# Two attention layers on one core: maxima run 40 units ahead instead of 36, and TensorE's program written out without a loop

## The reference

```
xn  = group_norm(x) * gamma + beta
qkv = w_qkv @ xn + b_qkv                      # per head q, k, v of 32 rows
m   = softmax_t( (q*scale)^T (k*scale) )      # 1024 x 1024 for each of 8 heads
a   = m @ v
out = x + w_proj @ a + b_proj                 # the second layer does the same with its own weights
```

## Time and profile before

| | us |
|---|---|
| median of 3 runs (2229.60 to 2244.59) | 2239.12 |
| the profiled execution | 2236.67 |
| its span, first to last instruction | 2234.9 |
| TensorE busy in the span | 2123.1 (95%) |
| GpSimd busy | 1790.2 (80%) |
| VectorE busy | 1700.2 (76%) |
| ScalarE busy | 1243.4 (56%) |
| mean granted TensorE clock (1 is 2.4 GHz) | 0.974 |

### The profile page before, as it was taken

One profiled execution on the slowest core, in us unless ns is written; L12 is line 12 of the kernel. 1 busy time (PEld: TensorE's weight loads), 2 busy tenths in 40 slices (PEclk: granted clock), 3 DMA queues, 4 the chain that ended last, 5 costly groups with the idle time before them and its releaser, 6 DMA issues.

```text
span 2234.9 us, 41842 instructions
## 1 busy us (share of the span) xinstructions
PE 2123.1 (95%) x10552; PEld 1156.9 (52%) x10552; DVE 1700.2 (76%) x2896; ACT 1243.4 (56%) x2321; POOL 1790.2 (80%) x567
## 2 busy tenths in 40 slices
PE   5999999999999999999999999999999999999998
PEld 2455555555555555455554555545455554555542
DVE  3788777787877778777877878877787787878872
ACT  2455656565555655555555555655556555565554
POOL 2498788797887988878987888978889788889885
PEclk8899999999999999999999999999999999999999
DMA  4332233422233332233312334322343222433210
GB/s 120 58 95 43 50 81 76 97 57 63 59 71 97 77 79 49 47 96 95 93 37 56 89 77 95 67 49 59 77 96 77 54 58 62 96 77 76 52 44 20
DMA packets 208771, 157.53 MB, mean 70 GB/s; under 512 B 166528, under 2 KB 166784, under 8 KB 208512
## 3 DMA queue, kind: packets, MB, share of 16 engines
q1 hardware_dynamic: 208512, 154.48, 30.2%
HBM read 36.39 MB, written 16.78 MB: 24 GB/s over the span
## 4 chain that ended last, share of the span: by engine, by line
PE 64%; SPq 23%; issue 4%; DMA 3%; POOL 3%; DVE 2%; ACT 1%; ACTq 0%; DVEq 0%; POOLq 0%
PE ps_t L390 16%; PE ps_v L436 15%; PE ps_m L415 14%; SPq L284 13%; PE ps_d L458 10%; SPq L294 7%; PE ps_m L450 4%; PE ps_d L473 4%; DMA qs<-neg_max 3%; POOL acc L870 2%; SPq L257 1%; DVE raw_max L702 1%; DVE stage_kl L719 1%; DVE res L769 1%; SPq L266 1%
## 5 line engine op out<-in xcount | busy, mean ns | idle before, releaser
L625 ACT ACTIVATE pt<-ps_t 128x512 f32<-128x512 f32 x2048 | 1114.5, 599 | 918.2 <-PE ps_t L390 909.8
L702 DVE TENSOR_REDUCE raw_max<-ps_m 128x1 f32<-128x512 f32 x2048 | 1318.2, 685 | 397.9 <-PE ps_m L415 391.8
L870 POOL TENSOR_TENSOR acc<-acc,pt 128x2048 f32<-128x2048 f32 x317 | 1450.0, 4574 | 33.0 <-POOL gn_c L855 5.5
L415 PE MATMUL ps_m<-ks,qs 96*128 96x512 f32 x2048 | 997.0, 488 | 8.0 <-DVE raw_max L702 7.4
L390 PE MATMUL ps_t<-qs,ks 97*128 97x512 f32 x2048 | 853.0, 418 | 77.1 <-DMA qs<-neg_max 55.7
L390 PEld LDWEIGHTS ps_t<-qs,ks 97*128 97x128 f32 x2048 | 393.0, 192 | 467.0 <-issue 194.6
L870 POOL TENSOR_TENSOR acc<-pt 128x2048 f32<-128x2048 f32 x64 | 292.5, 4570 | 352.6 <-ACT pt L625 352.6
L436 PE MATMUL ps_v<-pt,v 128*32 128x512 f32 x4096 | 511.7, 618 | 0.0
L415 PEld LDWEIGHTS ps_m<-ks,qs 96*128 96x128 f32 x2048 | 395.3, 193 | 175.3 <-DVE raw_max L702 93.6
L458 PE MATMUL ps_d<-xn,wq 128*128 128x512 f32 x500 | 267.8, 620 | 5.8 <-ACT xn L657 5.8
L436 PEld LDWEIGHTS ps_v<-pt,v 128*32 128x32 f32 x4096 | 115.9, 111 | 270.2 <-issue 206.6
(11 more groups left out here) (49 smaller groups left out, 533.9 us busy)
## 6 DMA issues: line engine op xcount, KB each, us to landing
ks<-stage_kh SPq DMA_DIRECT2D x256, 128.0 KB, 2.4
qs<-stage_qh SPq DMA_DIRECT2D x256, 128.0 KB, 2.4
ks<-stage_kl SPq DMA_DIRECT2D x128, 128.0 KB, 2.4
qs<-stage_ql SPq DMA_DIRECT2D x128, 128.0 KB, 2.5
qs<-neg_max SPq DMA_DIRECT2D x1024, 0.5 KB, 2.0
xn<-x_dram SPq DMA_DIRECT2D x16, 512.0 KB, 4.1
res<-x_dram SPq DMA_DIRECT2D x16, 512.0 KB, 4.2
between<-res SPq DMA_DIRECT2D x32, 256.0 KB, 2.1
```

Source lines behind the costliest of these rows:

```text
L415: pe.matmul(ps_m[max_bank(u)][:, :], qs[b][0:KROWS, h, c:c + P], ks[b][0:KROWS, h, kf * HALF:(kf + 1) * HALF], start=True, stop=True).then ...
L625: act.activation(pt[t % 4][:, h, :], ps_t[score_bank(s.g, u)][:, :], ACT.Exp, scale=SCALE).then_inc(exp_done, 1)
L702: dve.tensor_reduce(raw_max[:, e % 2, t, kf:kf + 1], ps_m[max_bank(u)][:, :], AX.X, ALU.max)\
L870: pool.tensor_tensor(acc[hf][:, :, :], a[:, :, :], pt[t % 4][:, :, :], ALU.add).then_inc(pool_added, 1)
```

## The change

LEAD goes from 4 to 8, so the maxima run 40 units ahead. ROWS_AT goes from 3 to 7, so SP's rounds carry rows 5, 6, 7 and then 0, 1, 2, 3, 4 of the next slot, and the first five rows are loaded before slot 0 instead of four. TensorE no longer calls `run_slots`: `write_slots` writes its 32 slots out one after the other. The other four engines keep their loops.

```diff
-LEAD = 4
+LEAD = 8
 AHEAD = NT * HG + LEAD
...
-ROWS_AT = 3
+ROWS_AT = 7
...
+def write_slots(slot):
+
+    for n in range(SLOTS):
+        slot(plain(n), first=n == 0, has_next=n + 1 < SLOTS, has_second=n + 2 < SLOTS, has_third=n + 3 < SLOTS)
...
-            for e in range(HG):
+            for e in range(AHEAD // MAX_GROUP):
                 load_row(e, 0, e)
...
-            run_slots(pe, slot)
+            write_slots(slot)
```

## The result

The changed kernel takes 2145.28 us (median of 4 runs, 2143.58 to 2149.15) against 2240.55 us (4 runs) before it on the same chip: the ratio is 0.9585, 95% interval 0.9547 to 0.9622. The profiled execution took 2149.15 us, 87.5 us less than the 2236.67 us of before. Forecast were 2157 us and 79.6 us less.

The account below looks back on a forecast made before the run. Bound: TensorE mostly, SP's DMA queue in places. From the profiled 2236.7 us, minus 55.7, 7.8 and 27.2, plus 3.0, 5.6 and 2.5, gave 2157.1; forecast 2157, own range 2143 to 2173, overall range 2138 to 2184.

Parts of the forecast that it names:

- row waits: TensorE's 30 waits for `neg_max` rows, late by their place in SP's queue, would go: 55.7 us gained.
- their restarts and low clock: On TensorE after late rows: 30 restarts of 0.26 us and 16 low-clock pieces of 1.7 us saved, 7.8 plus 27.2.
- closings: At six closings TensorE stands 3.2 us in unit 3, not 2.7 in unit 0; low clock stays: 3.0 us lost.
- fold's new place: On VectorE, fold, statistic and unit 24 in a row delay unit 27 in 14 odd slots: 5.6 us lost.
- start, four more maxima: In the prologue, four more maxima would cost 2.5 us.
- a wait of unit 3 for VectorE: At the start of slots 5, 9, ..., TensorE's unit 3 would wait for VectorE, 16 to 22 us in total.
- Rival A: TensorE's written-out program pays in full, as other engines' closings shorten without three fetching at once: 2128 us; chance 0.12.
- (B): TensorE's low clock stays and strikes elsewhere: 2184 us; chance 0.08.
- (C): GpSimd becomes the bound in odd slots' second halves, slipping 1 to 2 us each: 2178 us; chance 0.05.
- (D): Nothing moves, since another row is as late, say row 0 behind the fourth staging: 2236 us; chance 0.04.
- (E): TensorE's straight program stops at each of 114 fetched code blocks, 2.7 us each: 2465 us; chance 0.03.

Follow-up runs that it names:

- run on the statistic: The changed kernel with the first channel statistic of a block after unit 24 instead of 23; one execution, 2151.37 us.

## Why the prediction was right, step by step

The time lay 12 us under the forecast, inside the range and its own narrower one. Against the profiled time, 87.5 us gained for 79.6 forecast:

| step | forecast, us | in the traces, us |
|---|---|---|
| row waits | -55.7 | -55.3 |
| their restarts and low clock | -35.0 | -33.5 (none of the 16 low pieces left) |
| closings | +3.0 | -10.2 |
| fold's new place | +5.6 | +8.3 in slots 1 to 28 |
| start, four more maxima | +2.5 | +4.1 |
| slots 0, 30 and 31 otherwise | 0 | -0.9 |

The yardstick for the second and fourth steps is a slot with neither a row wait nor a closing nor a moved fold. The run with the row first has such slots. The first half of its slot 3, the whole of slot 3, and slot 6:

```profile
256.42:288.26 31.84, 31.84 (x175) 19.73 (x174) 27.23 (x48) 18.01 (x35) 27.52 (x7) 1.00 0.57 142
256.42:320.61 64.19, 64.13 (x339) 37.32 (x338) 54.06 (x94) 37.35 (x72) 54.63 (x23) 1.00 0.36 84
453.18:516.73 63.55, 63.55 (x322) 34.15 (x321) 52.02 (x89) 39.92 (x75) 57.69 (x14) 1.00 0.31 68
```

Fourteen odd slots of 64.19 and fourteen even ones of 63.55 are 1788.4 us. The kernel before takes 1898.3 for its slots 1 to 28, 109.9 more: 51.7 of row waits, 26.6 of closings, and 31.6 for the restarts and the low clock of the 28 waits there, 15 of which have a low piece. At 0.26 a restart, that leaves 1.6 us a low piece, where 1.7 was forecast; slots 0 and 30 bring it to 33.5. The changed kernel takes 1813.7, 25.3 more: 16.4 of closings, 0.6 in slot 1 with its late landing, and 8.3 for the folds.

*Rows:* right in mechanism and size. The row first brings nearly all of it with the data no earlier (1.7 us of waits left), and the longer lead without the new place brings none of it.

*Closings:* the mechanism was right in the main, the size not; this is the term mis-sized. Before, a closing cost 2.7 us and 1.7 of low clock, 26.6 us for six. Now it costs 67.3 - 64.6 = 2.7, 16.4 for six, where the forecast had 6 x (3.2 + 1.7) = 29.4. The 3.2 was too high: the fold kept VectorE back only to +1.35 (in slot 5), and reduction 0 started 3.2 us after it, so that TensorE went on at +5.3, and at +5.1 behind the later closings; the bounds were +5.1 and +6.1. The sign named for it, a wait of unit 3 for VectorE of 16 to 22 us in total, reads 13.2 us, and half of that is put down to ScalarE, whose closing ends sooner and which the forecast did not have in the wait. But with ScalarE written out VectorE's closing costs the same 2.7, so ScalarE's share adds nothing.

The larger part of the miss is the low clock, which I kept behind all six and which this trace shows behind none. The run on the statistic has it behind five of six. That is one execution of another kernel at a mean clock of 0.987; the changed kernel's other three executions read 0.992 to 0.994, no lower than the profiled one's 0.990. Two of them, at 0.994, come to 26 us of low clock each, and every trace here has at least 20 of that before slot 0. So at most one or two low pieces can stand behind their closings, and the forecast was wrong to count six. What decides it is open.

Rival A asked what the written-out program would bring in full, 29 us; alone it brought 8 to 10 (by the ratio and by the medians). Whether closings get shorter when they don't coincide is not shown: ScalarE idles 2.2 to 2.4 us in the changed kernel's closings, where VectorE branches 1.3 us after it, and 2.4 to 2.8 with the written-out program alone, where VectorE branches 0.3 us after it, but no run varied that distance by itself.

When VectorE's and ScalarE's loops go too, the time falls by 17 us (2145 to 2128). In the traces slots 1 to 28 get 22.9 us shorter by it: 16.4 are the six closings, 0.6 is slot 1, and 5.9 are folds that cost less; the last slot gives 2.2 back.

The Trainium skill, "Runtime: NRT & Kernel Launch", section "Instruction fetch mechanics", says that a taken branch can stall its engine and that kernels therefore prefer full unrolling. The traces agree for the engine itself: TensorE's 15.4 us under "issue" are gone. They show besides that the time comes in full only when the engines that close at the same place are unrolled together.

*Fold:* 0.33 us in each odd slot's first half (32.17 against 31.84 above) is 4.6; the even slots, where I saw slack, lose 0.10 or 0.27, 2.6 together; the second halves lose the remaining 1.1. I had counted only the odd ones.

*Start:* slot 0 starts at 79.0 instead of 74.9, but in the traces here it starts anywhere from 70 to 79, and at 74 in another kernel with the same lead, so 2.5 us cannot be read from it.

*The other rivals:* no low clock is left in slots 1 to 28 (B), GpSimd kept up (C), no other row came late (D), and straight TensorE code had no gap (E): slots 2 to 4, 6 to 8 and so on read 63.7 to 63.9 and 64.6 us, all busy.

So part of the closeness is luck: 13 us too much for the closings stand against 4 us too little for the folds and the start.

## What to carry to other kernels

When an engine waits for a DMA that was issued late, ask first whether its data or its place in the issuing queue was late: here a swap of two statements in SP's order, data no earlier, gave 3.8%, and data 3 units earlier without the swap gave nothing. A wait also costs what follows it, the clock above all: the 55.7 us of waits were worth 89. And take a loop off all engines that close together: here TensorE's alone brought 8 to 10 us; in the changed kernel VectorE's brought 11 more, ScalarE's and GpSimd's on top of it 6 more, and ScalarE's without VectorE's nothing.

## What the runs showed of the hardware

- **Issue time was the same at two sizes.** On SP's queue a DMA of 128 KB and one of 512 bytes both took about 0.6 us to issue, so 46 of them fill 29.5 us. With the row put first in that queue its waits went, so the queue, not the transfers, was the limit.
- **Landing.** The rows' DMAs landed 2.0 us after their issue began (median); in the changed kernel one took 6.7 us.
- **The closing of a loop.** In the traces TensorE shows 2.4 to 3.1 us of idle time at a closing, ScalarE 2.2 to 3.4, VectorE 2.9 to 3.6 (where TensorE closes too, the longer ones include waiting for TensorE's product), GpSimd none that can be seen (its additions ran on through each).
- **Granted clock.** In slots 1 to 28 of all the traces, single idle pieces of TensorE of 1.3 to 1.6 us had it at 1.2 GHz behind them in 2 of 17 cases, pieces of 2.0 us and more in 51 of 61, for 3.4 or 6.8 us. Two pieces of 0.9 to 1.3 us with work between them had it in none of six cases in the changed kernel and in five of six in the run on the statistic.
